# Scaling attention queries inside the exponential instead of beforehand

## The reference

```
q, k, v = split(x @ Wqkv)                      # 16 heads of 64
q = l2norm(q) * qs;  k = l2norm(k) * ksc       # t / max(|t|, 1e-12)
q = q*cos*scale + rotate_half(q)*sin*scale
k = k*cos/scale + rotate_half(k)*sin/scale
sim  = q @ k^T * 8, masked to a window of 32 tokens back
attn = softmax(sim);  out = (attn @ v) @ Wo + x
x = out + (a * gelu(gate)) @ W2 + b2           # with a layernorm ahead
```

## Time and profile before

| | us |
|---|---|
| three executions | 2259.07, 2266.51, 2268.06 |
| median | 2266.51 |
| the profiled execution | 2265.41 |
| its span, first to last instruction | 2263.6 |
| busy: PE, DVE, ACT, POOL | 2043.8, 1716.2, 1631.4, 1730.2 |
| mean granted TensorE clock | 0.974 of full speed |

### The profile page before, as it was taken

The page is one execution under the profiler, slowest core; times in us unless marked ns, Lnnn a source line. Parts: engine busy times, 40 slices in busy tenths (PEclk is TensorE's granted clock), DMA queues, the critical chain, the costliest instruction groups (busy, mean ns, idle before and its releaser), DMA issues.

```text
span 2263.6 us, 71089 instructions
## 1 busy us (share of the span) xinstructions
PE 2043.8 (90%) x23552; PEld 1539.0 (68%) x23552; DVE 1716.2 (76%) x4197; ACT 1631.4 (72%) x5654; POOL 1730.2 (76%) x1364
## 2 busy tenths in 40 slices
PE   5999939999989999889999899999899998899996
PEld 3666627777657777567777477776577775677772
DVE  3555568888678888678887688886788886888875
ACT  3555428888758888578887588887588885788872
POOL 3333449999689999589997699995799995899960
PEclk9999959999999999999999999999999999999998
DMA  2000012121121212032111212111212110221110
GB/s 68 2 0 0 4 49 83 43 55 42 39 69 43 56 42 49 18 85 48 50 42 43 64 45 53 44 42 39 70 43 53 44 42 24 54 54 44 42 41 19
DMA packets 40903, 98.67 MB, mean 44 GB/s; under 512 B 6480, under 2 KB 20432, under 8 KB 39856
## 3 DMA queue, kind: packets, MB, share of 16 engines
q1 hardware_dynamic: 40752, 96.75, 16.5%
HBM read 20.32 MB, written 1.05 MB: 9 GB/s over the span
## 4 chain that ended last, share of the span: by engine, by line
PE 30%; DVE 26%; issue 18%; ACT 17%; POOL 7%; DVEq 1%; POOLq 0%; ACTq 0%; DMA 0%; SPq 0%
ACT prob L478 10%; DVE n2c L796 6%; DVE n L789 5%; DVE ts_ L799 5%; ACT nat L494 4%; PE bank L1142 3%; DVE tc_ L792 3%; PE bank L1176 3%; DVE nmax L746 3%; PE bank L1149 3%; PE bank L1046 2%; ACT kT L516 2%; PE bank L1178 2%; PE bank L1177 2%; PE bank L1060 2%
## 5 line engine op out<-in xcount | busy, mean ns | idle before, releaser
L317 POOL TENSOR_TENSOR rn<-n2c,half_neg 128x8 f32<-128x8 f32 x384 | 633.2, 1649 | 127.3 <-DVE n2c L796 126.5
L478 ACT ACTIVATE prob<-bank,nmax 128x96 f32<-128x96 f32 x1536 | 502.6, 352 | 132.1 <-DVE nmax L746 131.9
L319 POOL TENSOR_TENSOR tsum<-tc_,ts_ 128x512 f32<-128x512 f32 x384 | 490.2, 1277 | 0.0
L322 POOL TENSOR_TENSOR w_nat<-tsum,rn 128x512 f32<-128x512 f32 x384 | 400.9, 1044 | 37.8 <-POOL tsum L319 15.1
L789 DVE TENSOR_REDUCE n<-nat 128x8 f32<-128x512 f32 x384 | 262.1, 683 | 142.2 <-ACT nat L494 139.5
L478 ACT ACTIVATION_READ_ACCUMULATOR prob<-bank,nmax 128x1 f32 x1536 | 333.1, 217 | 0.0
L1176 PE MATMUL bank<-w_hi,xs 128*128 128x512 f32 x576 | 277.4, 482 | 36.0 <-DVE ts_ L799 15.3
L799 DVE TENSOR_TENSOR ts_<-bank,ropeL 128x256 f32<-128x256 f32 x768 | 285.2, 410 | 0.0
L487 ACT ACTIVATE pT<-bank 96x512 f32<-96x512 f32 x384 | 230.8, 601 | 74.4 <-PE bank L1149 72.2
L494 ACT ACTIVATE nat<-bank 128x512 f32<-128x512 f32 x384 | 232.7, 606 | 70.4 <-PE bank L1178 67.5
L1149 PE MATMUL bank<-idf,prob 128*96 128x128 f32 x1536 | 245.0, 283 | 42.0 <-ACT kT L516 28.6
(11 more groups left out here) (129 smaller groups left out, 4059.0 us busy)
## 6 DMA issues: line engine op xcount, KB each, us to landing
vspace<-v_nat SPq DMA_DIRECT2D x96, 384.0 KB, 4.0
vspace<-v_nat SPq DMA_DIRECT2D x96, 256.0 KB, 3.4
vspace<-v_nat SPq DMA_DIRECT2D x95, 128.0 KB, 2.3
nat<-w_qkv SPq DMA_DIRECT2D x5, 1536.0 KB, 8.0
wo<-w_o SPq DMA_DIRECT2D x6, 512.0 KB, 4.0
w<-w SPq DMA_DIRECT2D x6, 341.0 KB, 3.0
shared<-w_qkv SPq DMA_DIRECT2D x1, 1536.0 KB, 6.7
w<-w SPq DMA_DIRECT2D x6, 192.0 KB, 3.1
```

The lines of the kernel that those rows point to most:

```text
L317: nc.gpsimd.tensor_tensor(rn[:, r, :], n2c[:, r, :], half_neg[:, 0:8], ALU.pow).then_inc(pool_step, 1)
L319: nc.gpsimd.tensor_tensor(tsum[:, r, :], tc_[:, r, :], ts_[:, r, :], ALU.add).then_inc(pool_step, 1)
L322: nc.gpsimd.tensor_tensor(w_nat[:, r, :].rearrange("p (h d) -> p h d", d=D), tsum[:, r, :].rearrange("p (h d) -> p h d", d=D), rn[:, r, :] ...
L478: last = nc.scalar.activation(prob[:, 4 * b + i, :], SB[b][:, i * SPAN:(i + 1) * SPAN], ACT.Exp, bias=nmax[:, p, 8 * G + 4 * b + i:8 * G + ...
```

## The change

The product with the inverse norm goes for the q steps (j = 0 and 2): POOL adds tc_ and ts_ straight into w_nat, and the power writes rnq, kept for two tiles. In ACT's exponentials rnq becomes the scale, an operand with one value per partition beside the bias. DVE's reductions write nraw, and two products 128x4 then multiply the maxima by rnq to give the bias. The k steps are as before. POOL's loop becomes one of two tiles, so that the buffer index p is a constant.

```diff
-            def rotate(q_idx):
+            def rotate(t, p):
                 for j in range(4):
-                    r, Q = j % 2, q_idx + j
+                    r, Q = j % 2, t * 4 + j
+                    cols = slice(4 * j, 4 * j + 8)
                     eng.wait_ge(n2c_ready, Q + 1)
-                    nc.gpsimd.tensor_tensor(rn[:, r, :], n2c[:, r, :], half_neg[:, 0:8], ALU.pow).then_inc(pool_step, 1)
+                    if r == 0:
+                        at_least(eng, p_ready, t * 4 - 4)
+                        nc.gpsimd.tensor_tensor(rnq[:, p, cols], n2c[:, r, :], half_neg[:, 0:8], ALU.pow).then_inc(pool_step, 1)
+                        eng.wait_ge(pj_dve, Q + 1)
+                        at_least(eng, tp_full, Q - 1)
+                        nc.gpsimd.tensor_tensor(w_nat[:, r, :], tc_[:, r, :], ts_[:, r, :], ALU.add).then_inc(w_ready, 1)
+                        continue
+                    nc.gpsimd.tensor_tensor(rn[:, :], n2c[:, r, :], half_neg[:, 0:8], ALU.pow).then_inc(pool_step, 1)
                     eng.wait_ge(pj_dve, Q + 1)
-                    nc.gpsimd.tensor_tensor(tsum[:, r, :], tc_[:, r, :], ts_[:, r, :], ALU.add).then_inc(pool_step, 1)
-                    eng.wait_ge(pool_step, Q * 2 + 2)
+                    nc.gpsimd.tensor_tensor(tsum[:, :], tc_[:, r, :], ts_[:, r, :], ALU.add).then_inc(pool_step, 1)
+                    eng.wait_ge(pool_step, t * 6 + (3 if j == 1 else 6))
...
                     last = nc.scalar.activation(
                         prob[:, 4 * b + i, :], SB[b][:, i * SPAN:(i + 1) * SPAN], ACT.Exp,
-                        bias=nmax[:, p, 8 * G + 4 * b + i:8 * G + 4 * b + i + 1], accum_out=lsum[:, p, head:head + 1])
+                        scale=rnq[:, p, head:head + 1], bias=nmax[:, p, 8 * G + 4 * b + i:8 * G + 4 * b + i + 1],
+                        accum_out=lsum[:, p, head:head + 1])
...
             def maxima(t, p, G):
                 for b in range(2):
                     eng.wait_ge(s_ready, t * 2 + (G + 1))
-                    nc.vector.tensor_reduce(nmax[:, p, 8 * G + 4 * b:8 * G + 4 * b + 4],
+                    nc.vector.tensor_reduce(nraw[:, 4 * b:4 * b + 4],
                                             SB[b][:, 0:4 * SPAN].rearrange("p (h k) -> p h k", h=4),
-                                            AX.X, ALU.max, negate=True).then_inc(max_ready, 1)
+                                            AX.X, ALU.max, negate=True).then_inc(raw_ready, 1)
+                for b in range(2):
+                    eng.wait_ge(raw_ready, t * 4 + (2 * G + b + 1))
+                    eng.wait_ge(pool_step, t * 6 + (1 + 3 * G))
+                    nc.vector.tensor_tensor(nmax[:, p, 8 * G + 4 * b:8 * G + 4 * b + 4], nraw[:, 4 * b:4 * b + 4],
+                                            rnq[:, p, 8 * G + b:8 * G + 8:2], ALU.mult).then_inc(max_ready, 1)
```

More of the change, by code:

```diff
@@ L112, in build @@
         n2c = sb("n2c", [P, 2, 8])
-        rn = sb("rn", [P, 2, 8])
+        rn = sb("rn", [P, 8])
+        rnq = sb("rnq", [P, 2, HEADS])
+        nraw = sb("nraw", [P, 8])
         tc_ = sb("tc_", [P, 2, HB])
         ts_ = sb("ts_", [P, 2, HB])
-        tsum = sb("tsum", [P, 2, HB])
+        tsum = sb("tsum", [P, HB])
         w_nat = sb("w_nat", [P, 2, HB])
@@ L168, in build @@
         tp_full, tp_free, prev_ready = sem("tp_full"), sem("tp_free"), sem("prev_ready")
+        raw_ready = sem("raw_ready")
         s_ready, max_ready, p_ready = sem("s_ready"), sem("max_ready"), sem("p_ready")
@@ L310, in pow_rstd @@
                 nc.gpsimd.tensor_tensor(rstd[:, :], veps[:, :], half_neg[:, :], ALU.pow).then_inc(ln_pow, 1)
-            def rotate(q_idx):
+            def rotate(t, p):
                 for j in range(4):
-                    r, Q = j % 2, q_idx + j
+                    r, Q = j % 2, t * 4 + j
+                    cols = slice(4 * j, 4 * j + 8)
                     eng.wait_ge(n2c_ready, Q + 1)
-                    nc.gpsimd.tensor_tensor(rn[:, r, :], n2c[:, r, :], half_neg[:, 0:8], ALU.pow).then_inc(pool_step, 1)
+                    if r == 0:
[6 more added lines that the diff above has]
+                    nc.gpsimd.tensor_tensor(rn[:, :], n2c[:, r, :], half_neg[:, 0:8], ALU.pow).then_inc(pool_step, 1)
                     eng.wait_ge(pj_dve, Q + 1)
-                    nc.gpsimd.tensor_tensor(tsum[:, r, :], tc_[:, r, :], ts_[:, r, :], ALU.add).then_inc(pool_step, 1)
-                    eng.wait_ge(pool_step, Q * 2 + 2)
+                    nc.gpsimd.tensor_tensor(tsum[:, :], tc_[:, r, :], ts_[:, r, :], ALU.add).then_inc(pool_step, 1)
+                    eng.wait_ge(pool_step, t * 6 + (3 if j == 1 else 6))
                     at_least(eng, tp_full, Q - 1)
                     nc.gpsimd.tensor_tensor(
-                        w_nat[:, r, :].rearrange("p (h d) -> p h d", d=D), tsum[:, r, :].rearrange("p (h d) -> p h d", d=D),
-                        rn[:, r, :].rearrange("p (h o) -> p h o", o=1).to_broadcast([P, 8, D]), ALU.mult).then_inc(w_ready, 1)
+                        w_nat[:, r, :].rearrange("p (h d) -> p h d", d=D), tsum[:, :].rearrange("p (h d) -> p h d", d=D),
+                        rn[:, :].rearrange("p (h o) -> p h o", o=1).to_broadcast([P, 8, D]), ALU.mult).then_inc(w_ready, 1)
             pow_rstd(0)
@@ L377, in _ @@
             begin(eng, 3)
-            rotate(0)
+            rotate(0, 0)
             def layer(l, last):
-                with eng.Fori(1, TILES) as n:
-                    rotate((n + l * TILES) * 4)
+                rotate(l * TILES + 1, 1)
+                with eng.Fori(1, TILES // 2) as i:
+                    rotate(i * 2 + l * TILES, 0)
+                    rotate(i * 2 + (l * TILES + 1), 1)
                 for s in range(SUPERS):
@@ L393, in layer @@
                     tables(l + 1)
-                    rotate((l + 1) * TILES * 4)
+                    rotate((l + 1) * TILES, 0)
             with eng.Fori(0, DEPTH - 1) as l:
```

## The result

The changed kernel takes 2575.8 us (median of 4; 2570.0 to 2580.7), the kernel before 2266.5: a ratio of 1.137, 95% interval 1.133 to 1.142. It is slower by 309 us. The forecast was 2615, with a range of 2450 to 2700. The profiled execution took 2570.0 us, 304.6 more than that of before.

The account below looks back on a forecast made before the run. Bound: the ring of hand-overs on ACT's timeline (A to D, 17.08 us a tile), not POOL's work. Items 1 to 4 gave +3.70 us per tile, +333, plus 17 for closing tiles: +350 on 2265.4, 2615 us; range 2450 to 2700.

Parts of the forecast that it names:

- B: Part of a tile on ACT's timeline, from exponentials (0,0) to the end of copy kT of j3: 5.28 us.
- C: Hand-over after B: PE's transposes and scores, DVE's maxima, until exponentials (1,0) start; 2.50 us, called latency.
- D: ACT from exponentials (1,0) through square j3, after a 0.47 us wait for PE, to kT of j1: 6.29 us.
- A: Same hand-over as C, to the next tile's exponentials: 3.01 us, 0.56 less in the other tile of the pair.
- POOL's freed time decides: Rival: added latency in the tile loop lies beside other work, so the kernel gets faster, 2223 us; chance 0.06.
- Item 1: POOL loses two products per tile, so the wait for PE in D goes: -0.47 us per tile.
- Item 2: 16 exponentials in B and D get a second per-partition operand at 0.09 us each: +1.44 us per tile.
- Item 3: In A and C, both maxima and a product now precede the exponentials: 0.70 us each, +1.40 us per tile.
- Item 4: The product reads two SBUF tensors and waits for POOL: 0.93 in C, 0.4 in A, +1.33 us per tile.
- No port wait: Rival: the small product in A and C slips in or arrives beside POOL's power: 2496 us; chance 0.16.
- The second operand is hidden: Rival: the exponentials' added operand hides behind the accumulator read after each: 138 us less, 2477; chance 0.12.
- The sums cancel: Rival: the loop's gains and losses cancel, or something unseen sets its timing: within 0.5%; chance 0.04.

Follow-up runs that it names:

- run 1: Changed kernel without the exponentials' scale and without the new products, maxima straight from the reductions; queries' inverse norms applied nowhere: 2238.3 us.
- run 2: Changed kernel without the second operand of the exponentials; the two products stay but multiply by ones, so queries are unnormalised: 2320.4 us.
- run 4: Changed kernel, same result, with the reductions writing raw maxima to PSUM, so the product reads one SBUF tensor instead of two: 2421.6 us.
- run 8: Kernel before the change, same result, with the clamp n2c made as a maximum reduction over pairs (sum, 1e-24): 2222.3 us.
- run 3: Changed kernel with a column of ones as the exponentials' second operand and without the products, released as before; queries unnormalised: 2328.0 us.
- run 5: Changed kernel, same result, with each product directly behind its own reduction, so the first one releases the first exponentials: 2460.3 us.
- run 7: Changed kernel with the first group's 32 value matmuls done twice, the same result written again, where PE idles 1.64 us: 2532.5 us.

## Why the prediction was right

*What bounds the kernel: right.* The growth of the four parts accounts for the whole difference: over all tiles of the two profiled executions B takes 53 us more, C 135, D 38 and A 72, the closing tiles with what lies between the layers 7, together the 304.6 measured, within rounding. POOL's 2.08 us per tile were worth 0.29 (run 1), while the rival "POOL's freed time decides" needed nearly all of the added latency to stay off the ring. One reading of the rows was wrong, without an effect on the sum: the second tile of the pair is shorter by 0.56 us, of which A is 0.51; the rest is in B.

*Item 1, -0.47 us.* In size too large by itself: POOL's relief alone gives 0.29, because 0.20 of the wait stays. With the later exponentials the rest went too (D 5.56 in run 2, 0.74 less), which I had not counted. That is the slack into which the other terms partly fell.

*Item 2, +1.44 us.* The operand costs what was said: 442 against 352 ns, starts 0.41 apart against 0.32. On the ring B took 0.58 and 0.65 of its 0.72, since a gap of about 0.1 us in front of square j0 was there to fill, and D showed -0.02 for my +0.72 - 0.47. The Trainium skill, "ScalarE: Activation LUTs", section "What ACT_TABLE_LOAD costs", gives 93 ns; the rows give 90. The accumulator read that follows doesn't hide it, as the starts 0.41 us apart show.

*Item 3, +1.40 us.* Mis-sized: each hand-over grew by 0.54, not 0.70 (run 4: C 3.04, A 3.04 and 3.54). The product takes 0.16 us as taken. The Trainium skill, "VectorE: DVE Perf Modes", section "The TRN2 errata", has a formula for an fp32 addition of two tensors with N elements a partition, (N + 151)/0.96 ns, checked there for N = 512 and 2048. Carried to N = 4, as an estimate, it gives 161 ns: the medians of 158 (run 4) and 162 (changed kernel) agree. But instructions on DVE that don't need each other overlap by 0.08 to 0.09 us, and I added their lengths: the first product starts 0.93 to 0.94 us after the first reduction, ends 1.09 to 1.10 after it, and in the kernel before the first release came at 0.55.

*Item 4, +1.33 us.* Right in kind and place: 0.96 in C (0.93 was worked out) and 0.43 in A of one tile of the pair (0.41). In the other tile the 0 to 1.0 was 0; I took 0.4 for both, measured 0.22. Mean 1.18. Run 4 shows that the second SBUF input is the cause. The Trainium skill ("GPSIMD Engine Reference", section "Key points") names DVE instructions in a 2-port perf mode or with two SBUF inputs. The second half agrees with the traces: the product with two SBUF inputs takes up to 1121 ns (changed kernel), and the one with a PSUM input at most 164 (run 4). Whether the clamp with a constant, which takes up to 1282 ns (before), falls under the first half isn't shown, since no trace names the mode of an instruction; the reduction in its place takes at most 164 (run 8).

*The sum.* A regular tile went from 16.80 to 19.63 us, the mean of A's two values taken: +2.83, not +3.70. Some 0.32 of the difference is item 3, 0.15 item 4, and 0.40 lie in items 1 and 2, where the waits in B and D took more. Over 90 tiles +2.83 is 255; with the 17 for closing tiles as worked out, not measured apart, it is 272. The irregular tiles add 37. That is 309 for 304.6 measured. The forecast of 350 was high by 78 in its terms and low by 37 for the clock, for which I had written "I count no change": that sentence was wrong. The two errors pull against each other, so that the total is nearer than its terms; this part is luck. Without the fall of the clock the terms as measured would give 2265 + 272 = 2537.

*The signs.* The exponentials, their spacing, ACT's waits, the long products and POOL's 13.8 us per tile came as written. The regular tile, 19.6 us, lies a little below the 19.8 to 20.8 that I gave; the mean of all is 20.1.

*The rivals.* "No port wait" would have been 2496; run 4 is a kernel of that kind, and it takes 2422. "The second operand is hidden" is refuted by the row of the exponentials and by run 3, 90 us above run 1. "The sums cancel" and "faster" are refuted by the time.

## What to carry to other kernels

An engine that is busy for 96% of a loop is not its bound unless the chain goes through its work: here 200 us of POOL's work were worth 8 us once its hold on the shared port was gone, and that hold, felt by the clamp, 44. Before a scaling is moved off a busy engine, count the hand-overs it is put into: two small instructions between scores and exponentials, and an operand on each of 16 small instructions, cost more than the 512-wide products that they replaced. Look also at tiny vector instructions beside a busy GpSimd (POOL): here one with a constant or with two SBUF inputs took up to eight times its length, and one with a PSUM input, or made as a reduction, never did.

## What wasn't expected of the hardware

- A DVE product of 128x4 takes 147 to 164 ns alone and up to 1121 ns beside POOL; how long depends on where in POOL's addition it arrives. An arrival earlier by 0.5 us took C from 4.00 to 2.79 us and A from 3.5 to 3.85 (run 5).
- Behind an idle time of PE of 1.64 us inside a dense stream the granted clock fell to 0.50 in 27 of 90 tiles and not in the others; filling that time with matmuls nobody needs made the kernel 43 us faster (run 7). What decides between the two is left open. The length of the idle time alone isn't it: in 57 more tiles of the changed kernel it is 1.56 to 1.66 us as well, and in run 5 another one of 1.5 to 1.6 us stands in 39 places, all with a clock of 1.00 behind it.
- The clamp's wait at the port, which the kernel before already had, was worth 44 us (run 8), more than the relief of POOL by 192 products (28 us, run 1).
